# A four-layer perceiver kernel: query products of the first attention by one head and four tiles, and all eight key tiles of the last attention made in the merged middle

## The reference, cut to what matters

```python
x = x + L0_xattn(layernorm(x), ctx, Wq, Wk, Wv, Wo)     # 32 query heads, 4 key heads of 128, keys = context and x
x = x + L0_ffn(layernorm(x), ...)                       # dense product and 28 low-rank experts
x = x + L1_xattn(layernorm(x), ctx, mask, ...)          # 32 query heads, 8 key heads, RMS norms of q and k
x = x + L1_ffn(layernorm(x), ...)                       # dense product and 8 experts
x = x + L2_xattn(layernorm(x), ctx, ctx)                # linear attention: softmax(q) @ (softmax(k).T @ v)
x = x + L2_ffn(layernorm(x), ...)                       # 4 experts
x = x + L3_xattn(layernorm(x), ctx, Wq, Wk, ...)        # one head of 512, K = rmsnorm(rmsnorm(ctx) @ Wk.T + bk)
x = x + L3_ffn(layernorm(x), ...)                       # clustered product
```

## Time and profile before

| | |
|---|---|
| median of 3 runs | 1513.99 us (1512.72 to 3684.55) |
| the profiled execution | 1514.85 us, its span 1513.1 us |
| mean granted TensorE clock | 0.992 |
| TensorE busy | 1472.1 us of the span (97%) |
| VectorE, ScalarE, GpSimd busy | 1032.4, 926.9, 402.4 us |

### The profile page before, as it was taken

The page is one execution under the profiler, slowest core; times in us unless marked ns, Lnnn a source line. Parts: engine busy times, 40 slices in busy tenths (PEclk is TensorE's granted clock), DMA queues, the critical chain, the costliest instruction groups (busy, mean ns, idle before and its releaser), DMA issues.

```text
span 1513.1 us, 27936 instructions
## 1 busy us (share of the span) xinstructions
PE 1472.1 (97%) x9532; PEld 1316.5 (87%) x9532; DVE 1032.4 (68%) x2449; ACT 926.9 (61%) x3133; POOL 402.4 (27%) x461
## 2 busy tenths in 40 slices
PE   8999999999999999998999999999999999989997
PEld 7999999999999998887888888888888888877885
DVE  7556555655565557886777777777777788767776
ACT  4456455545564555547777777777777774466652
POOL 5112011301130102233232323232323242644431
PEclk9999999999999999999999999999999999989999
DMA  5000100010000100101111110101010101011101
GB/s 219 33 29 29 43 29 29 29 43 29 29 29 29 43 29 27 57 35 43 36 43 42 37 50 29 50 29 50 29 50 29 39 8 67 29 46 37 48 15 60
DMA packets 16115, 62.60 MB, mean 41 GB/s; under 512 B 2228, under 2 KB 3764, under 8 KB 10984
## 3 DMA queue, kind: packets, MB, share of 16 engines
q1 hardware_dynamic: 15976, 60.82, 11.5%
HBM read 58.72 MB, written 2.10 MB: 40 GB/s over the span
## 4 chain that ended last, share of the span: by engine, by line
PE 54%; issue 26%; DVE 9%; ACT 6%; POOL 4%; DMA 0%; SPq 0%; POOLq 0%; ACTq 0%; DVEq 0%
PE psY L958 12%; PE psQ L874 9%; PE psKV L898 7%; PE psSO L843 2%; PE psSO L945 2%; POOL wo L541 2%; PE psTP L859 2%; PE psTP L908 2%; PE psQ L859 1%; PE psQ L799 1%; PE psSO L844 1%; PE psTP L928 1%; PE psKV L814 1%; ACT prob L1487 1%; PE psQ L1245 1%
## 5 line engine op out<-in xcount | busy, mean ns | idle before, releaser
L958 PE MATMUL psY<-wo,oT 128*128 128x512 f32 x1536 | 378.2, 394 | 0.7 <-DVE oT L1943 0.2
L958 PEld LDWEIGHTS psY<-wo,oT 128*128 128x128 f32 x1536 | 278.8, 188 | 56.2 <-POOL wo L541 2.2
L541 POOL TENSOR_TENSOR wo<-stage_o,wo 128x512 fp32r<-128x512 f32 x68 | 87.2, 1313 | 310.3 <-ACT wo L1400 279.6
L1400 ACT ACTIVATE pT<-psTP 64x256 fp32r<-64x256 f32 (+1 forms) x192 | 86.5, 451 | 124.2 <-PE psTP L928 123.4
L1490 ACT ACTIVATE prob<-wide,neg_mx 128x128 f32<-128x128 f32 x256 | 99.7, 391 | 81.5 <-DVE neg_mx L2075 81.5
L1487 ACT ACTIVATE prob<-s_sb,neg_mx 128x64 f32<-128x64 f32 x256 | 85.9, 337 | 94.2 <-DVE neg_mx L2075 94.2
L1943 DVE TENSOR_TENSOR pT<-psTP,pT 64x256 fp32r<-64x256 f32 (+1 forms) x192 | 97.6, 508 | 67.3 <-ACT pT L1400 65.5
L665 POOL TENSOR_TENSOR rms<-ms_eps,minus_half 128x5 f32<-128x5 f32 (+1 forms) x64 | 74.2, 1159 | 230.6 <-DVE ms_eps L2088 229.8
L541 POOL TENSOR_TENSOR wq<-stage_q,wq 128x512 fp32r<-128x512 f32 x42 | 53.9, 1301 | 209.3 <-ACT wq L1400 156.6
L898 PEld LDWEIGHTS psKV<-wkv,arena 128*128 128x128 f32 x768 | 100.3, 190 | 6.8 <-DVE kT L2123 1.8
L874 PE MATMUL psQ<-wq,hT 128*128 128x512 f32 x384 | 103.8, 407 | 0.0
(11 more groups left out here) (329 smaller groups left out, 3489.9 us busy)
## 6 DMA issues: line engine op xcount, KB each, us to landing
stage_o<-in_wo SPq DMA_DIRECT2D x16, 1024.0 KB, 4.8
stage_q<-in_wq SPq DMA_DIRECT2D x15, 1024.0 KB, 5.1
stage_kv<-in_wkv SPq DMA_DIRECT2D x12, 512.0 KB, 3.6
stage_q<-in_ctx SPq DMA_DIRECT2D x16, 256.0 KB, 3.0
stage_o<-in_ctxT SPq DMA_DIRECT2D x2, 1024.0 KB, 4.8
stage_q<-in_base SPq DMA_DIRECT2D x2, 1024.0 KB, 4.9
stage_kv<-in_ctx SPq DMA_DIRECT2D x8, 256.0 KB, 3.0
out<-x_res SPq DMA_DIRECT2D x8, 256.0 KB, 2.2
```

The lines of the kernel that those rows point to most:

```text
L541: g.tensor_tensor(dst[LO], stage, dst[HI].bitcast(f32), ALU.subtract).then_inc(ld[done or what + "_lo"], 1)
L958: m = mm(psY[:], oT[:, ol, h, :], wo[:, wl, h, :], start=h == 0 and i == 0, stop=h == HQ - 1 and i == 2)
L1400: copy = lambda o, i: nc.scalar.activation(o, i, ACT.Copy)
```

## The change

Four things are changed, with the buffers that they need.

1. Units 8 to 55 of the first attention (six head groups) cover one head and four tiles: 12 matmuls of 512 columns. Units 0 to 7 and 56 to 63 stay as they were.
2. A unit is computed three steps ahead: steps 4 and 6 compute two units each, steps 53 and 54 none. The copies (`units_kept`) are made in pairs in the even steps: the first where it was, the second behind the exponentials on ScalarE and behind `normalise` on VectorE, and none in the odd steps. The next group's query weights are made at t = 5, 12, 20, ..., 52 in place of 6, 14, ..., 54, and the key weights at 14, 30, 46 in place of 12, 28, 44.
3. `heads_of_four` is one buffer at the top of the on-chip memory for the kept queries; kT1, v1, qT and, over its end, xn lie in it. Two layer norms use q_sb where they used xn.
4. The middle makes key tile n = t-5: all eight tiles, at t = 5 to 12. Tiles 0 to 3 go through psQ and psY, 4 to 7 through psE and psKT. A key is normalised in place in stage_q's fourth slot, so the context ring there has three slots. The last attention makes none.

```diff
-    def units_of(st):
-        first = [st] if st.static and st.t == 0 else []
-        return first + [st.back(-1)] * st.back(-1).exists
+    def units_of(t):
+        early = {0: (0, 1), 1: (2,), 2: (3,), 3: (4,), 4: (5, 6), 5: (7,), 6: (8, 9), 7: (10,), 8: (11,)}
+        if t.t > STEPS - NT - 4:
+            return [unit(t.t + 1)] if STEPS - NT <= t.t + 1 < STEPS else []
+        return [unit(k) for k in early.get(t.t, (t.t + 3,))]
+    def units_kept(t):
+        early = {0: (0, 1), 1: (), 2: (2, 3), 3: (4,), 4: (5, 6), 5: (7,)}
+        if t.t > STEPS - NT - 4:
+            return units_of(t)
+        return [unit(k) for k in early.get(t.t, () if t.t % 2 else (t.t + 2, t.t + 3))]
...
             def q_unit(k):
                 need(pe, s["qT_lo"], k.t - 1)
...
+                    parts = [(unit_bank(k)[:].rearrange("p (n t) -> p n t", n=4), k.t % 4)]
+                for out, h in parts:
...
                 if t1.exists:
                     exps(t1)
+                for k in units[1:]:
+                    unit_hi(k)
...
                 if t1.exists:
                     normalise(t1)
+                for k in units[1:]:
+                    unit_lo(k)
...
         def k_product(n):
-            need(pe, N3["k_in"], n)
+            if n < 4:
+                pe.wait_ge(LNS[5]["lo"], ln_at(5, n + 2))
...
         def k_transpose(n):
             pe.wait_ge(N3["kn"], n + 1)
-            need(pe, N3["kT_lo"], n)
+            if n < 4:
+                pe.wait_ge(M["x_add"], n + 4)
...
         def middle_step(t):
-            s, f, e, n = M, FF[2], t - 5, t - 9
+            s, f, e, n = M, FF[2], t - 5, t - 5
...
                     need(pe, LNS[5]["lo"], ln_at(5, t - 4))
+                    if 0 < n < 5:
+                        pe.wait_ge(N3["k_in"], n)
...
-                if p < 4:
-                    if p == 0:
-                        pe.wait_ge(FS["x_add"], 3 * NT)
-                    k_product(p + 4)
```

More of the change, by code:

```diff
@@ L501, in _ @@
                 load("wkv", stage_kv[:, :, 2 * P:4 * P], io["b2"], 28)
[L502 to L509, removed]
+            if n >= 3:
+                sp.wait_ge(M["e_tr"], n - 2)
+            sp.dma_start(stage_q[:, n % 3], io["ctx"][:, n]).then_inc(ld[f"slot{n % 3}"], 16)
+            if n == 5:
+                load("wkv", stage_kv[:, :, 2 * P:4 * P], halves_of(row_of("bk3")), 31)
+                load("wkv", stage_kv[:, :, 0:128], io["cent"], 31)
+                sp.wait_ge(ld["wo_lo"], 71)
+                for j, what in enumerate(("kn3", "qn3")):
+                    sp.dma_start(stage_o[:, j], row_of(what)).then_inc(ld["fn_in"], 16)
         sp.wait_ge(M["e_tr"], NT)
@@ L640, in power @@
         def power(what, n, col):
+            if what == "k":
+                pool.wait_ge(N3["k_sq"], n + 1)
+                need(pool, N3["kn"], n)
+                g.tensor_scalar(small[:, 4:5], small[:, 7:8], 1.0 / D, RMS_EPS3, ALU.mult, ALU.add).then_inc(N3["ms_k"], 1)
             pool.wait_ge(N3["ms_" + what], n + 1)
@@ L738, in _ @@
         middle_step(4)
-        low_wk(0)
         for t in range(5, NT + 5):
@@ L1002, in attention @@
                         kv_proj(t)
-                    if t1.exists and units:
+                    if t1.exists and not ending:
                         scores(t1)
@@ L1497, in unit_hi @@
                 act.wait_ge(s["q_units"], k.t + 1)
-                need(act, s["scores"], k.t - 2 + k.res(2))
+                need(act, s["scores"], scores_before(k.t))
                 copy(unit_in(HI, k), unit_out(k)).then_inc(s["qT_hi"], 1)
@@ L1561, in attention @@
                 next_wo = a.rms and t.res(8) == 2 and t.t < STEPS
-                units = [] if a.rms else units_of(t)
-                scores_first = not a.rms and not units
+                units = [] if a.rms else units_kept(t)
+                scores_first = not a.rms and t.t >= STEPS - 1
                 if scores_first:
@@ L1569, in attention @@
                     squares(t)
-                changes_wq = not a.rms and t.exists and t.res(8) == 6 and t.t < LN_SLOT
-                if changes_wq:
+                new_wq = not a.rms and changes_wq(t)
+                if new_wq:
                     next_wq(t, 0, 1)
@@ L1579, in attention @@
                     squares(t)
-                for k in units[:-1]:
-                    unit_hi(k)
+                if t.t == 0 and units:
+                    unit_hi(units.pop(0))
                 if a.index == 0 and t.static and t.t == 0:
@@ L1598, in attention @@
                     scores_lo(t1)
-                for k in units[-1:]:
+                for k in units[:1]:
                     unit_hi(k)
@@ L1602, in attention @@
                     next_wq1(t)
-                if changes_wq and not early:
+                if new_wq and not early:
                     next_wq(t, 2, 3)
@@ L1628, in attention @@
                     high_wo(0)
-                if not a.rms and t.res(16) == 12 and t.exists:
+                if not a.rms and t.t in (14, 30, 46, 60):
                     act.wait_ge(s["kv"], t.div(16) * 8 + 8)
-                    if t.static and t.t == 60:
+                    if t.t == 60:
                         high_wkv(4, 504)
@@ L2202, in attention @@
                     gates(FF[1], 0)
-                for k in units[:-1]:
-                    unit_lo(k)
+                if t.t == 0 and units:
+                    unit_lo(units.pop(0))
                 between = first if t.static and t.t == 0 else ()
@@ L2219, in attention @@
                     row_max(t1)
-                for k in units[-1:]:
+                if a.norm_slot(t) and not a.rms and not scores_first:
+                    ln_norm(next_ln, t.t - LN_SLOT)
+                for k in units[:1]:
                     unit_lo(k)
@@ L2228, in attention @@
                     k_normalise(t)
-                if t.exists and not a.rms and t.res(8) == 6 and t.t < LN_SLOT:
+                if not a.rms and changes_wq(t):
                     low_wq(t.div(8) + 1, 3)
```

235 lines of the change are left out of this document (124 added, 111 removed).

## The result

The changed kernel takes 1525.84 us (median of 7 runs, 1523.35 to 1530.92), the kernel before beside it 1516.18 (median of 7, one of which took 3684.55). The ratio is 1.0073, with a 95% interval of 1.0064 to 1.0083: slower by 0.7%. The profiled execution took 1525.84 us, with a span of 1524.1 us, 11.0 more than before. The forecast was 1518.5, within 1502 to 1533; the direction was right and the size (4.5 us) was less than half of what came (9.7 by the medians). The measured time lies in the band from 1522 to 1534 that the prediction had given to its second rival, the slow clock.

A forecast was written before the change was run, and what follows sets the result against it. TensorE was taken to bound both attentions, the VectorE and ScalarE chain the middle. 1514.85 + 3.8 (first attention) - 10.5 (last) + 11.2 (middle) = 1519.4, or 1518.5 by the runs' median, 0.9 lower; range 1502 to 1533 us.

The forecast's parts named there:

- second rival: Middle steps 6 to 9 fall to 1.2 GHz after a wait of about 2.7 us: +10 to +13, 1530 us; chance 0.15.
- Units of 512 columns: First attention: a unit takes 2.75 us instead of 2.88, gaining 0.13; 39 units give -5.1 us.
- The second copy: First attention: a pair's second copy delays six steps with output weights by 0.6 us each, +3.6 us.
- Steps 53 and 54: First attention: without units, TensorE waits for probabilities, then the keys' copy: 2.6 and 2.0 us, +4.6 us.
- The stage as a whole: First attention: all its gains and losses together were forecast at +3.8 us, within -2.5 and +9.
- The middle: Steps 5 to 9 with the added key tiles: 52.7 us in place of 41.5, +11.2 us, within +2.5 and +16.
- the ring: Middle, through psQ: k_product waits for layer norm 5's low part, which waits on k_read; one turn 11.8 us in step 7.
- The last attention: Four key tiles less save 13.0 us, of which waits bring some back: -10.5 us, within -13.0 and -7.
- own range: Whole kernel: the main forecast's range, 1512 to 1522 us, given chance 0.45.
- wide range: Whole kernel: 1502 to 1533 us, covering the forecast and its rivals, with 0.05 beyond either end.
- Rival 1: Middle follows TensorE as queues overlap better: +2.5 there, whole 1504 to 1509, say 1507 us; chance 0.25 with its neighbourhood.
- Rival 3: First attention: 512 columns save nothing at 240 ns each, so +8.9 there and 1524 us overall; chance 0.10.

The follow-up runs named there:

- units_split: The kernel before with only the change's first attention, each product of 512 columns made as two of 256: 1525.86 us, 1.0066 against the kernel before.
- units_late: The kernel before with only the change's first attention, each pair's second copy placed later on ScalarE and VectorE: 1515.93 us, 1.0008 against the kernel before.
- middle_norm_first: The kernel before with only the change's middle and last attention, layer norm 5's copy and low part placed earlier: 1517.77 us, 1.0010 against the kernel before.
- before_value_early: The kernel before, with VectorE making the value norm between the gates' two halves in middle steps 5 to 7: 1511.58 us, 0.9981 against the kernel before.
- last_tuned: middle_norm_first with the last layer norm's transposes and copies earlier at p = 0 and GpSimd's low part later at p = 3: 1515.94 us, 1.0014 against before.
- change_repaired: The full change with the edits of units_late, middle_norm_first and last_tuned: 1517.76 us, 1.0016 against the kernel before.

## Why the prediction was right and wrong

**Units of 512 columns: right.** A gain of 0.13 us per unit was forecast, and the units and `units_split` show 0.11 to 0.13. By the Trainium skill's gap that the prediction cites ("TensorE: Matmul & The Clock Gate", section "Back-to-back issue gap") all 48 would have given 1.5 us; the split costs 5.2 over 46 of them, so the rows decide against it for these streams.

**The second copy: right in its place, too dear in its size.** Six steps with output weights were to lose 0.6 us each. Against before, the steps behind them lose 0.47 us each where there are keys and 0.34 where there are none, 2.4 in all in place of 3.6. For the three with keys `units_late` shows that it is the copy, 0.5 us each; for the three without, the copy was in the way in that run too, and the cause stays argued.

**Steps 53 and 54: right in kind, short by the clock.** 4.6 us were forecast. The waits measure 4.0 us, for the probabilities and then for the keys' low part, as named. By the starts of the output products from step 52 to step 55, with the two missing units (5.8 us) added, the two steps cost 6.4: step 54 costs 2.1, where 2.0 was forecast, and step 53 costs 4.4, where 2.6 was. What was not in the sum is the slow product behind step 53's waits, 1.5 us. The stage as a whole came out at +4.1 for a forecast of +3.8, and that is luck: steps 6 to 52 gained 2.7 us in place of 1.2, which made up for the 1.8 too much in steps 53 and 54.

**The middle: the sizes fit, the reason holds for one step, the clock was left out of the sum.** Forecast for steps 5 to 9: 8.8, 11, 11.8, 11.8 and 9.3 us, sum 52.7. Measured: 9.5, 12.8, 11.2, 13.4 and 8.9, sum 55.9. The slow stretches in steps 6 and 8 cost about 1.6 us each; without them it is 9.5, 11.3, 11.2, 11.9 and 8.9, sum 52.8. No step is off by more than 0.7, and the errors cancel. The mechanism, the norm's low part behind the gates, is shown by `middle_norm_first` for step 8, for the 0.9 us in front of step 5's product and for 0.5 us of step 7. In step 6 the product doesn't wait for that low part at all, and cutting the ring doesn't move the step; the long wait in steps 6 and 7 is the 1.27 us for the key's norm, which the prediction didn't name. That these two sizes came out is luck.

The step that failed is the choice between forecast and second rival: the rival asked for a wait of about 2.7 us in one piece and was priced as all or nothing, at 10 to 13 us. What came was a third of it: 3.4 us at 1.2 GHz in step 6 and 3.4 in step 8, the latter behind a wait of 2.41, and some 3.1 us of cost, all but 0.1 of what the middle is over its forecast. The rival's price rested on one execution of before; the same wait in the other kernels with the old middle was followed by 6.8, 3.4 or 0 us at 1.2 GHz.

**The last attention: cover undervalued.** -10.5 was forecast, -7.3 came. The terms were 13.0 less 1.3 for the first query transposes, 1.0 for the similarity at p = 3 and 0.2 elsewhere. The first measured 2.1. The query's copy ended 1.2 us after TensorE was free, about as forecast, but a layer norm's low part, which the prediction hadn't looked at, came 0.8 later; the key tile that stays behind at p = 0 has its transposes and copies ahead of that norm's, on three engines. At p = 3 the similarity waits 0.7, and 1.4 stand in front of the probabilities' transpose, which had no wait in the forecast; 0.9 of them is GpSimd's instruction beside VectorE's. p = 2 and p = 4 have 0.7 and 0.5, against 1.0 us in the same steps before. Together the waits rise by 4.5 us in place of 2.5; 1.2 us more of the difference isn't assigned to a row.

**The sum.** 1519.4 + 0.3 (first attention) + 3.2 (middle) + 3.2 (last attention) = 1526.1; the profiled execution took 1525.84. The forecast's own range, 1512 to 1522, missed it; the wide range held it, as its upper part was made for the clock. About half of the miss is the clock and half is the last attention, which came out at the end of its bounds (-7). Rival 1 (the holes take the keys, +2.5 us in the middle) failed as argued: with the ring cut, steps 5 to 9 take 49.5 us against 41.5, and with the waits of 1.27 us gone too, 46.1. Rival 3 is excluded by the split.

## What to carry to other kernels

When work is moved off a TensorE-bound stage, price it by the waits that it covered there and not by its own length: of the 13 us taken out of the last attention, 7.3 were gained. Where a chain through slower engines will leave TensorE idle in one piece, as in step 8 (2.41 us), put part of the price of a slow stretch (some 1.6 us for each 3.4 where TensorE is the bound) into the forecast itself, not into a rival alone. And look at what stands between an available input and its copy in the in-order queues: moving one piece of work a few places was worth 2.6 us (`units_late`), 5.3 (`middle_norm_first`) and 2.8 (`before_value_early`). Check in the trace where the wait went: in `last_tuned` and `before_value_early` a part of it came back one instruction or one product later.

## What the runs showed of the hardware

But for the one at the program's end, stretches at 1.2 GHz lasted 3.4, 6.8 or 10.2 us in these traces. Where TensorE was busy throughout, 3.4 us cost 1.5 to 1.6. Whether one came could not be read from the program or the wait. Step 53 in `units_late` and in `change_repaired`, with the same copies:

```profile
517.54 0.66 PE L982 MATMUL psTP<-ident,prob 128*128 128x128 f32 x4 [1.52 <-DVE prob L2137]
518.47 3.14 PE L952 MATMUL psKV<-wkv,hT 128*128 128x256 f32 x24 [0.27 <-DVE arena L1999]
...
519.16 0.66 PE L988 MATMUL psTP<-ident,prob 128*128 128x128 f32 x4 [1.53 <-DVE prob L2139]
520.10 4.65 PE L958 MATMUL psKV<-wkv,hT 128*128 128x256 f32 x24 [0.28 <-DVE arena L2001]
```

The first stays at full clock, the second has 3.4 us at 1.2 GHz. The wait of 1.91 to 1.94 us in step 3 is in all seven kernels with the new first attention, and four of them have a slow stretch behind it. The 2.14 us in the last attention had none in any of the three traces that hold it. So two traces that differ in a slow stretch don't show that the edit between them made or removed it. The executions of one kernel spread over 3 to 8 us from the fastest to the slowest, and a trace alone doesn't settle a difference of 2 us.

VectorE's scaling of a 128x128 tile in SBUF took 1.25 us while a GpSimd subtraction of 1.26 us ran, and 0.29 once that stood behind it; then the VectorE instruction that ran beside it (128x512, two tiles as inputs) took 1.83 in place of 0.75. The Trainium skill ("SBUF — State Buffer", section "SBUF: two separate sides") says that VectorE and GpSimd share a pair of SBUF ports by an exclusive lock, held for a whole instruction, against VectorE's two-port modes and its instructions with two SBUF inputs. By that rule the scaling can't end before GpSimd's instruction, and it ends just behind it: 1438.94 + 1.25 = 1440.19, against 1438.85 + 1.26 = 1440.11. The trace agrees, and so do the 1.83 us. It doesn't show in which mode the scaling ran, and the 0.08 us behind GpSimd's end are fewer than the 0.29 that the scaling takes alone.
